# Spreading routing weights by one f32r product per slot, and a split wait in the feed-forward blocks

## Chip, cores and metric

One core of one Trainium2 chip. The metric is the device time of one execution in microseconds (us), measured three times for the kernel before. The five engines are TensorE (PE, with its weight loads shown as PEld), VectorE (DVE), ScalarE (ACT), GpSimd (POOL) and SyncE (SP). Each runs its own instructions in order and waits for others by semaphores.

## The reference

Four layers stand behind each other, each with a layer norm and added to its input: windowed attention, a feed-forward network (FFN) with routed low-rank parts, a state-space mixer, and the same FFN again. x has 1024 tokens of 256 values. The FFN is what the change touches:

```python
gate_logits = einsum('bsd,ed->bse', x, gate_w)          # 8 experts
topw, sel = top_k(gate_logits, 2)
topw = softmax(topw, axis=1)                            # over the tokens, not over the two
base_up, base_gate = xt @ w_up.T, xt @ w_gate.T         # 704 hidden
for e in range(8):
    c = sum(where(sf == e, wf, 0.0), axis=1)            # weight of a token for this expert
    h_e = silu(base_up + lo_up[e]) * (base_gate + lo_gate[e])   # lo_*: rank 16
    ch = c[:, None] * h_e
    mixed_h += ch
    lora_down += 2.0 * (ch @ down_A[e].T @ down_B[e].T)
out = mixed_h @ w_down.T + lora_down
```

Everything is float32.

## The kernel before

The kernel doesn't loop over experts: each token has two slots (its two chosen experts), and all work is done for slot 0 and slot 1. Values lie transposed, with hidden units on the 128 partitions and tokens in the columns, in two halves of 512 tokens (HALF). The 704 hidden units are HB = 6 blocks; the last is half full, and its up and gate products share one bank. So an FFN has N = 12 steps i = 6 * half + block. Precision is kept by splitting each float32 operand in a high and a low f32r part and adding three products (`three`).

What a step does, by engine:

- PE: `base_x(i)` makes the up products (6 of 512 columns, into bank i % 2) and the gate products (6 more, into bank 2 + i % 2); for the half-full block there is one group of 6. `base_lora(i)` adds the low-rank part of slot 0 (3 + 3 products), then signals `a`. `second(i)` adds, on top, the low-rank part of slot 1 less that of slot 0, once slot 0 has been read (`t0`), and signals `b`. `down(i)` is the product with the down weights.
- ACT: `silu(i, s)` reads the up bank into f_sil (signals `sil0`, `sil1`), and copies high parts.
- DVE: `gated(i, s)` multiplies the gate bank with f_sil into f_t (signals `t0`, `t1`); then f_t times the routing weight f_wb gives f_ch; low parts are differences. In the first FFN, ACT and DVE also split the weights as they come in (`split`, pieces 0 to 7; block b needs piece b + 1).

The steps overlap. The queue of PE in iteration i is `base_x(i)`, `base_lora(i)`, `second(i - 1)`, `down(i - 2)`; `base_x(i)` waits for `t1` of step i - 2, which used the same banks. After the loop, PE goes on with early products of the mixer.

The start of an FFN is written out by hand. The masks of slot 0 and slot 1 (`masked(h, n)`, n = 0 to 7: 0 to 3 for slot 0, 4 and 5 for the up part of slot 1, 6 and 7 for its gate part) are multiplied by DVE into f_um and counted by `um`. Between them, DVE, PE and ACT hand each other the steps of the softmax over the tokens; it ends with DVE's WT, one column for each pair of slot and group of 128 tokens, with the tokens on the partitions. The weight of each token is wanted in all partitions, along the columns. `weigh(h)` on PE does that, with WT's column repeated as the stationary operand and the identity as the moving one, four products of 128 columns for each slot and half, in plain float32. ACT copies the result from PSUM to f_wb (`weights_out`). `weigh(0)` stands behind `second(0)`, `weigh(1)` behind `base_x(2)`.

The mixer later in the program does a thing of the kind the change brings: it repeats a small tile over 128 columns, splits it (tile cumsum_hl) and has POOL scale it by parameter columns (L2014, L2022).

Of the kernel before, what the change touches and what calls it, by code (L numbers as in the profile page):

```python
# [20 lines left out]
F32 = mybir.dt.float32  # L21
# [63 lines left out]
PR_END = PR_CS + 26  # L85
# [17 lines left out]
def build(nc, ins, out, phases=4):  # L103
    ctx = ExitStack()
    with ctx:
# [166 lines left out]
        def attention():  # L272
# [511 lines left out]
            def banks_free(e):  # L784
# [22 lines left out]
        F_EVENTS = dict(lg=2, lgt=2, lgr=2, lgc=2, m8=NT, ix=NT, ixf=2, hot=4, top_dve=6, top_pe=3, ex=SLOTS,  # L807
                        wb=4, wbc=4, u=4, uhi=4, ulo=4, mk=4, mk0=2, mk1=2, mk2=2, um=16,
                        da=4, dd0=4, dd=4, dh=4, dl=4, y=4, add=4)
        F_EVENTS |= {n: 2 * HB for n in "a b d sil0 sil1 t0 t1 ch0 ch1 mix mxh mxl".split()} | dict(chh=4 * HB, chl=4 * HB)  # L810
        FS = {n: sem(f"ffn_{n}") for n in F_EVENTS}
        TOP_DVE = {n: i + 1 for i, n in enumerate(("mt", "gm", "dg", "nmc", "rs", "wt"))}
        TOP_PE = {n: i + 1 for i, n in enumerate(("mtT", "nm", "sum"))}

        def ffn(tag, first, before):
# [16 lines left out]
            d_hl = at(f"{tag}_d_hl", [P, 2, HALF], F32R, U_CH + 18432)  # L832
            lg = small[:, 0:64]
# [5 lines left out]
            WT = sm[:, 32:48].rearrange("p (k t) -> p k t", k=2)  # L839
# [137 lines left out]
            def base_x(e, i, parts=(0, 1)):  # L977
# [22 lines left out]
            def pe(e):  # L1000
                def second(i):
                    h, b = divmod(i, HB)
                    if b == 0:
                        need(e, "um", 8 * h + 8)
                    need(e, "t0", i + 1)
                    for which in range(2):
                        m = three(e, to_bank(i, which), lambda w: blk(w, b, (FB_UPB, FB_GTB)[which]),
# [30 lines left out]
                base_lora(e, 0)  # L1038
                base_lora(e, 1)
# [60 lines left out]
            def act(e):  # L1100
# [26 lines left out]
                split(3)  # L1127
                a_hi(1, (0,))
# [14 lines left out]
                a_hi(1, (1,))  # L1143
                silu(0, 0)

# [1069 lines left out]
```

## Time and profile before

| | us |
|---|---|
| three timed runs, median (lowest, highest) | 546.32 (546.05, 546.5) |
| the profiled execution | 543.31 |
| its span, first to last instruction | 541.5 |
| busy PE, DVE, ACT, POOL | 517.0, 402.6, 310.8, 127.1 |

The span starts with the attention; the first FFN runs from 206 to about 330 us, the mixer to about 420, the second FFN to the end, with overlaps. The granted TensorE clock is 1.0 of full speed in every slice. Rows of the trace give the start and the duration in us, then engine, source line, operation, tiles written and read; "x12" means that twelve instructions in a row are merged in one row. In brackets stand the engine's idle time before and who ended it. Ends of PE's instructions overlap the next ones, so the distance from start to start is what an instruction costs there.

### The profile page before, as it was taken

What the parts mean: (1) busy time and instruction counts of PE and PEld (TensorE: products, weight loads), DVE (VectorE), ACT (ScalarE), POOL (GpSimd) and SP (SyncE); (2) the same over time, 40 slices, a digit from 0 to 9 for tenths busy, and PEclk for the clock granted to TensorE, in tenths of its full rate; (3) what the DMA queues carried; (4) which work ended last, traced back from release to release, by engine and by line L of the source; (5) the groups of instructions that cost most, each with busy time, mean ns of one, the idle gap of its engine ahead of it and who ended that gap; (6) DMA issues with size and microseconds to landing.
All of it is one profiled execution on the core that took longest, in us unless ns stands there. A gap on an engine that the chain in (4) does not pass through costs nothing. (4 is left out here: it accounts for less than half of the span.)

```text
span 541.5 us, 9132 instructions
## 1 busy us (share of the span) xinstructions
PE 517.0 (95%) x3035; PEld 436.8 (81%) x3037; DVE 402.6 (74%) x899; ACT 310.8 (57%) x768; POOL 127.1 (23%) x272
## 2 busy tenths in 40 slices
PE   5999999999999989999999999999898999999996
PEld 4778899998998977788887888757777778888885
DVE  5625565566566898799987899966886877898767
ACT  3656878588687643573443455889662254443342
POOL 2232424244243310000000004569533100000000
PEclk9999999999999999999999999999999999999999
DMA  7320100000002204000040000000000000000101
GB/s 273 116 79 1 40 2 2 2 0 2 2 2 70 83 1 142 1 1 1 0 137 0 2 1 0 2 0 2 0 1 2 0 1 1 1 1 0 40 1 39
DMA packets 5790, 14.25 MB, mean 26 GB/s; under 512 B 624, under 2 KB 2928, under 8 KB 5744
## 3 DMA queue, kind: packets, MB, share of 16 engines
q1 hardware_dynamic: 5744, 13.66, 7.3%
q8 instruction: 25, 0.41, 0.3%
q14 instruction: 21, 0.17, 0.1%
HBM read 12.61 MB, written 1.05 MB: 25 GB/s over the span
## 5 line engine op out<-in xcount | busy, mean ns | idle before, releaser
L170 PE MATMUL psum<-xT_hl,ffn_w_hl 128*128 128x512 f32 x312 | 77.7, 395 | 0.6 <-DVE f_t L1243 0.4
L170 PE MATMUL psum<-f_um,ffn_w_hl 128*128 128x512 f32 x288 | 72.2, 398 | 1.3 <-DVE f_t L1243 1.3
L170 PEld LDWEIGHTS psum<-xT_hl,ffn_w_hl 128*128 128x128 f32 x312 | 56.2, 188 | 12.2 <-issue 0.9
L170 PEld LDWEIGHTS psum<-f_um,ffn_w_hl 128*128 128x128 f32 x288 | 53.3, 188 | 14.2 <-DVE f_um L1255 2.1
L1140 ACT ACTIVATE f_sil<-psum 128x512 f32<-128x512 f32 (+1 forms) x48 | 28.6, 596 | 60.3 <-PE psum L170 60.0
L170 PE MATMUL psum<-wo_hl,oT_hl 128*128 128x256 f32 x384 | 50.8, 281 | 4.2 <-DVE oT_hl L705 2.6
L699 DVE TENSOR_TENSOR pT_hl<-psum,pT_hl 126x360 fp32r<-126x360 f32 (+1 forms) x44 | 23.6, 537 | 41.4 <-ACT pT_hl L606 41.4
L170 PEld LDWEIGHTS psum<-wo_hl,oT_hl 128*128 128x128 f32 x384 | 47.9, 188 | 7.1 <-DVE oT_hl L705 5.1
L170 PE MATMUL psum<-xT_hl,wq_hl 128*128 128x512 f32 x192 | 52.1, 407 | 0.6 <-ACT qT L572 0.6
L1243 DVE TENSOR_TENSOR f_t<-psum,f_sil 128x512 f32<-128x512 f32 (+1 forms) x48 | 33.2, 691 | 26.2 <-ACT f_sil L1140 25.4
L572 ACT ACTIVATE qT<-psum 128x512 f32<-128x512 f32 x32 | 35.0, 1094 | 29.0 <-PE psum L170 29.0
L1158 ACT ACTIVATE f_ch_hl<-f_ch 128x512 fp32r<-128x512 f32 x48 | 30.2, 630 | 37.0 <-DVE f_ch L1299 36.9
L581 ACT ACTIVATE probs<-probs,small 120x66 f32<-120x66 f32 x120 | 40.7, 349 | 4.2 <-DVE small L682 3.4
L170 PEld LDWEIGHTS psum<-xT_hl,wq_hl 128*128 128x128 f32 x192 | 33.9, 189 | 7.7 <-issue 1.7
L170 PEld LDWEIGHTS psum<-ffn_w_hl,f_mix_hl 128*128 128x128 f32 x288 | 36.8, 188 | 3.3 <-DVE x_resid L1342 1.2
L170 PE MATMUL psum<-f_ch_hl,ffn_w_hl 128*128 128x512 f32 x144 | 37.9, 397 | 0.6 <-DVE f_ch_hl L1310 0.6
L170 PE MATMUL psum<-ffn_w_hl,f_mix_hl 128*128 128x256 f32 x288 | 37.7, 280 | 0.5 <-DVE x_resid L1342 0.5
L755 POOL TENSOR_TENSOR probs_wide<-probs,small 120x186 f32<-120x186 f32 x40 | 20.0, 499 | 65.8 <-DVE small L662 65.5
L224 POOL TENSOR_TENSOR ln_rstd<-ln_var_eps,minus_half 128x4 f32<-128x4 f32 x8 | 8.1, 1012 | 113.9 <-DVE ln_var_eps L217 113.9
L1299 DVE TENSOR_TENSOR f_ch<-f_t,f_wb 128x512 f32<-128x512 f32 x48 | 33.2, 691 | 1.4
L170 PEld LDWEIGHTS psum<-f_ch_hl,ffn_w_hl 128*128 128x128 f32 x144 | 26.6, 188 | 7.0 <-DVE f_ch_hl L1310 1.0
L1310 DVE TENSOR_TENSOR f_ch_hl<-f_ch,f_ch_hl 128x512 fp32r<-128x512 f32 x48 | 31.1, 686 | 0.0
(242 smaller groups left out, 1121.4 us busy)
## 6 DMA issues: line engine op xcount, KB each, us to landing
w_raw<-in_wq SPq DMA_DIRECT2D x4, 512.0 KB, 3.3
w_raw<-in_wo SPq DMA_DIRECT2D x4, 512.0 KB, 3.3
ffn_w_raw<-in_ffn SPq DMA_DIRECT2D x3, 576.0 KB, 5.6
ffn_w_raw_far<-in_ffn SPq DMA_DIRECT2D x3, 576.0 KB, 5.2
ssd_w_raw<-in_ssd SPq DMA_DIRECT2D x3, 512.0 KB, 5.7
x_resid<-in_x SPq DMA_DIRECT2D x2, 512.0 KB, 4.4
out_x<-x_resid SPq DMA_DIRECT2D x4, 256.0 KB, 2.2
w_raw<-in_wk SPq DMA_DIRECT2D x1, 512.0 KB, 6.3
```

The lines of the kernel that those rows point to most:

```text
L170: i = e.matmul(dst, lhs(a), rhs(b), start=start and n == 0, stop=stop and n == len(TERMS) - 1, **kw)
L224: e.tensor_tensor(rstd[:, seg], veps[:, seg], minus_half[:, seg], ALU.pow).then_inc(LN["rstd"], 1)
L572: e.activation(qT[:, HALF * half:HALF * half + HALF, h], bank(7 if n == Q_PAIR else 6), ACT.Copy, scale=float(HD) ** -0.5).then_inc(s_qt, 1)
L581: m = e.activation(p[:, n, :], p[:, n, :], ACT.Exp, bias=NEGM[0:rows, u % 4, n:n + 1], accum_out=DEN[0:rows, u % 4, n:n + 1])
L699: e.tensor_tensor(pT_hl[0:nk, u % 2, LO, 0:n], bank(2 + u % 2)[0:nk, 0:n], f32(pT_hl[0:nk, u % 2, HI, 0:n]), ALU.subtract).then_inc(s_plo, 1)
L755: e.tensor_tensor(wide, p[:, :, SINK:KBLK], spread(r, KB_WIN), ALU.mult)
L1140: e.activation(sil[at_rows, s, :], bank(i % 2)[rows, :], ACT.Silu).then_inc(FS[f"sil{s}"], 1)
L1158: e.activation(ch_hl[:, i % 2, s, HI, :], ch[:, i % 2, s, :], ACT.Copy).then_inc(FS["chh"], 1)
L1243: e.tensor_tensor(tt[rows, s, :], to_bank(i, 1)[rows, :], sil[rows, s, :], ALU.mult).then_inc(FS[f"t{s}"], 1)
L1299: e.tensor_tensor(ch[:, i % 2, s, :], tt[:, s, :], wb[:, s, half(h)], ALU.mult).then_inc(FS[f"ch{s}"], 1)
L1310: e.tensor_tensor(ch_hl[:, i % 2, s, LO, :], ch[:, i % 2, s, :], f32(ch_hl[:, i % 2, s, HI, :]), ALU.subtract).then_inc(FS["chl"], 1)
```

## The change

`weigh` no longer makes eight plain float32 products for a half, but one f32r product of 512 columns for each slot. What it needs is made in new steps: DVE writes the 16 weight columns eight times beside each other (`w_rep`, 128x128). PE transposes that into bank 7, so that tokens lie in the columns and each partition holds one pair of slot and token group, repeated. ACT copies it rounded to f32r (`wr`), and DVE puts the low part into every other quarter of 32 partitions. ACT (half 0) and POOL (half 1) scale it by parameter columns that keep a partition's row only for its own token group (`wr_rhs`). The stationary operand (`slot_rows`) keeps the rows of a slot, so that the product sums high and low part over the partitions into all 128 of them. `pack` adds ten parameter columns.

DVE's queue at the start changes: `masked(0, 4, 5)`, then the new low part, `gated(0, 0)`, and only then `masked(0, 6, 7)`; `second(0)` waits for masks 4 and 5 before its up products and for 6 and 7 before its gate products. `base_x(i)` no longer waits for `t1` before all of its products, but before the up products for `sil1` of step i - 2 (except where that step is the half-full block) and before the gate products for `t1`.

In the mixer, two semaphores are merged into others to make room, with the counts moved on.

```diff
@@ events
-        TOP_DVE = {n: i + 1 for i, n in enumerate(("mt", "gm", "dg", "nmc", "rs", "wt"))}
-        TOP_PE = {n: i + 1 for i, n in enumerate(("mtT", "nm", "sum"))}
+        TOP_DVE = {n: i + 1 for i, n in enumerate(("mt", "gm", "dg", "nmc", "rs", "wt", "wlo"))}
+        TOP_PE = {n: i + 1 for i, n in enumerate(("mtT", "nm", "sum", "wT"))}
@@ base_x (PE)
-                if i >= 2:
-                    need(e, "t1", i - 1)
                 for which in parts[:1] if b == HB - 1 else parts:
+                    if i >= 2:
+                        need(e, "t1" if which or (i - 2) % HB == HB - 1 else "sil1", i - 1)
                     for k in range(KB):
@@ second (PE)
-                        need(e, "um", 8 * h + 8)
+                        need(e, "um", 8 * h + 6)
                     need(e, "t0", i + 1)
                     for which in range(2):
+                        if b == 0 and which:
+                            need(e, "um", 8 * h + 8)
@@ weigh (PE)
-                    need(e, "top_dve", TOP_DVE["wt"])
+                    need(e, ("wr0", "wr1")[h], 1)
                     if h:
                         need(e, "wbc", 2)
                     for s in range(SLOTS):
-                        for i in range(HT):
-                            t = HT * h + i
-                            m = e.matmul(bank(wb_bank(h, s))[:, i * P:(i + 1) * P],
-                                         WT[:, s, t:t + 1].broadcast_to([P, P]), ident, start=True, stop=True)
-                        m.then_inc(FS["wb"], 1)
+                        e.matmul(bank(wb_bank(h, s)), slot_rows[:, s, :], wr_rhs[:, h].rearrange("p t n -> p (t n)"),
+                                 start=True, stop=True).then_inc(FS["wb"], 1)
@@ pe
                 base_lora(e, 0)
+                need(e, "top_dve", TOP_DVE["wt"])
+                e.transpose(bank(7)[:, 2 * P:3 * P], w_rep, ident).then_inc(FS["top_pe"], 1)
                 base_lora(e, 1)
                 second(0)
                 weigh(0)
@@ act
                 split(3)
+                for n in range(SLOTS):
+                    e.activation(slot_rows[:, n, :], ones, ACT.Copy, scale=par[:, WR_SLOT + n:WR_SLOT + n + 1])
                 a_hi(1, (0,))
@@ act
                 a_hi(1, (1,))
+                need(e, "top_pe", TOP_PE["wT"])
+                e.activation(wr, bank(7)[:, 2 * P:3 * P], ACT.Copy).then_inc(FS["wrh"], 1)
                 silu(0, 0)
+                need(e, "top_dve", TOP_DVE["wlo"])
+                for t in range(HT):
+                    m = e.activation(wr_rhs[:, 0, t, :], f32(wr), ACT.Copy, scale=par[:, WR_HALF + t:WR_HALF + t + 1])
+                m.then_inc(FS["wr0"], 1)
@@ dve
-                e.tensor_tensor(WT, EX, spread(RS, NT), ALU.mult).then_inc(FS["top_dve"], 1)
-                masked(0, 4, 5, 6, 7)
+                copies = P // (SLOTS * NT)
+                wide = [P, copies, SLOTS, NT]
+                e.tensor_tensor(w_rep.rearrange("p (q k t) -> p q k t", q=copies, k=SLOTS),
+                                EX.rearrange("p (o k) t -> p o k t", o=1).broadcast_to(wide),
+                                RS.rearrange("p (o k u) -> p o k u", o=1, u=1).broadcast_to(wide),
+                                ALU.mult).then_inc(FS["top_dve"], 1)
+                masked(0, 4, 5)
+                need(e, "wrh", 1)
+                e.scalar_tensor_tensor(out=wr, in0=f32(wr), scalar=par[:, CS_LO:CS_LO + 1], in1=bank(7)[:, 2 * P:3 * P],
+                                       op0=ALU.mult, op1=ALU.add).then_inc(FS["top_dve"], 1)
                 gated(0, 0)
+                masked(0, 6, 7)
                 split(3)
                 gated(0, 1)
@@ pool
                 ln["rstd"](e, 1)
+                need(e, "top_dve", TOP_DVE["wlo"])
+                for t in range(HT):
+                    m = e.tensor_scalar(wr_rhs[:, 1, t, :], f32(wr), par[:, WR_HALF + HT + t:WR_HALF + HT + t + 1], None,
+                                        ALU.mult)
+                m.then_inc(FS["wr1"], 1)
@@ mixer (one of several places of the kind)
-                e.tensor_copy(second(HI), f32(second(LO))).then_inc(S["dtw"], 1)
+                e.tensor_copy(second(HI), f32(second(LO))).then_inc(S["wl"], 1)
...
-                                AX.X, ALU.add).then_inc(S["dtv"], 1)
-                e.wait_ge(S["dtv"], 1)
+                                AX.X, ALU.add).then_inc(S["dt_dve"], 1)
+                e.wait_ge(S["dt_dve"], 1)
```

## Rows read from the trace of the kernel before

**Rows 1.** PE's waits (total, times, longest); a window: length, busy PE, PEld, DVE, ACT.
```profile
PE psum L170 <- DVE f_t L1243: 1.8, 3, 0.7
...
237.00:246.00 9.00, 9.00 (x46) 7.55 (x45) 8.77 (x20) 4.91 (x9) 0.00 (x0) 1.00 0.00 0
```

**Rows 2.** Timeline of PE: start, us, engine, line, what, count, idle before.
```profile
223.17 3.05 PE L170 MATMUL psum<-f_um,ffn_w_hl 128*128 128x512 f32 x12
...
226.88 1.64 PE L170 MATMUL psum<-f_um,ffn_w_hl 128*128 128x512 f32 x6 [0.66 <-DVE f_t L1243]
...
230.06 3.01 PE L170 MATMUL psum<-xT_hl,ffn_w_hl 128*128 128x512 f32 x12
...
232.91 1.95 PE L1018 MATMUL psum<-const_f,softmax_small 128*128 128x128 f32 x16
...
234.61 3.04 PE L170 MATMUL psum<-f_um,ffn_w_hl 128*128 128x512 f32 x12
...
439.54 1.63 PE L170 MATMUL psum<-f_um,ffn_w_hl 128*128 128x512 f32 x6 [0.66 <-DVE f_t L1243]
```

**Rows 3.** Shapes of the new steps: timeline rows and, without a start, groups by form.
```profile
223.55 0.18 DVE L1283 TENSOR_TENSOR softmax_small<-softmax_small 128x16 f32<-128x16 f32 x1
...
350.88 0.35 DVE L1884 SCALAR_TENSOR_TENSOR cumsum_hl<-cumsum_hl,params,psum 128x128 fp32r<-128x128 f32 x1
...
219.63 0.27 PE L1031 MATMUL psum<-const_f,softmax_small 128*2 128x128 f32 x1
...
L1809 ACT ACTIVATE b_tok<-psum 128x128 f32<-128x128 f32 x8 | 2.2, 271 | 0.0
...
376.07 1.30 ACT L1826 ACTIVATE state_decayed<-state,ssd_small 128x128 f32<-128x128 f32 x4
...
L2014 POOL TENSOR_SCALAR cumsum_rhs<-cumsum_hl,params 128x128 fp32r<-128x128 f32 x4 | 1.7, 452 | 0.2 <-DVE ssd_small L1886 0.2
```

**Rows 4.** Timeline of ACT and DVE around block 0 of the first FFN.
```profile
223.64 2.49 DVE L1255 TENSOR_TENSOR f_um<-f_us,f_mT 128x512 fp32r<-128x512 f32 x4
...
224.85 0.60 ACT L1140 ACTIVATE f_sil<-psum 128x512 f32<-128x512 f32 x1 [0.32 <-PE psum L170]
226.05 0.69 DVE L1243 TENSOR_TENSOR f_t<-psum,f_sil 128x512 f32<-128x512 f32 x1
226.65 1.35 DVE L878 TENSOR_TENSOR ffn_w_hl<-ffn_w_raw,ffn_w_hl 128x1152 fp32r<-128x1152 f32 x1
...
228.56 0.60 ACT L1140 ACTIVATE f_sil<-psum 128x512 f32<-128x512 f32 x1 [3.10 <-PE psum L170]
229.19 0.69 DVE L1243 TENSOR_TENSOR f_t<-psum,f_sil 128x512 f32<-128x512 f32 x1 [1.19 <-ACT f_sil L1140]
```

**Rows 5.** Timeline of POOL and DVE in the mixer.
```profile
369.61 1.57 POOL L1971 TENSOR_SCALAR xs_D<-xs,params 128x512 f32<-128x512 f32 x1
...
372.81 1.05 POOL L2046 TENSOR_TENSOR x_dt_decay<-x_dt,decay 128x512 f32<-128x512 f32 x1
...
373.48 0.94 DVE L1908 TENSOR_TENSOR g_lo<-gated,g_hi 128x512 fp32r<-128x512 f32 x1 [1.87 <-ACT g_hi L1838]
373.84 2.00 POOL L1971 TENSOR_SCALAR xs_D<-xs,params 128x512 f32<-128x512 f32 x1
```

**Rows 6.** Timeline, further on in both FFNs: DVE's gaps and PE's next waits.
```profile
236.04 0.69 DVE L1318 TENSOR_TENSOR f_mix_hl<-f_mix,f_mix_hl 128x512 fp32r<-128x512 f32 x1 [0.31 <-ACT f_mix_hl L1169]
...
253.62 0.69 DVE L1243 TENSOR_TENSOR f_t<-psum,f_sil 128x512 f32<-128x512 f32 x1 [0.45 <-ACT f_sil L1140]
...
271.77 0.69 DVE L1243 TENSOR_TENSOR f_t<-psum,f_sil 64x512 f32<-64x512 f32 x1
...
272.91 2.89 PE L170 MATMUL psum<-xT_hl,ffn_w_hl 128*128 128x512 f32 x12
...
300.75 3.00 PE L170 MATMUL psum<-xT_hl,ffn_w_hl 128*128 128x512 f32 x12 [0.43 <-DVE f_t L1243]
...
457.94 0.69 DVE L1243 TENSOR_TENSOR f_t<-psum,f_sil 128x512 f32<-128x512 f32 x1 [2.18 <-ACT f_sil L1140]
```

More of the change, by code:

```diff
@@ L84 @@
 CS_LO, CS_RA, CS_RB, CS_LA, CS_LB, CS_FIRST = (PR_CS + n for n in (0, 1, 5, 9, 17, 25))
-PR_END = PR_CS + 26
+PR_WR = PR_CS + 26
+WR_HALF, WR_SLOT = PR_WR, PR_WR + NT
+PR_END = PR_WR + NT + SLOTS
 GW_PARTS = 2 * KB * EXPERTS
@@ L832, in ffn @@
             d_hl = at(f"{tag}_d_hl", [P, 2, HALF], F32R, U_CH + 18432)
+            wr = at(f"{tag}_weight_rows", [P, P], F32R, A_W + 16384)[:, :]
+            w_rep = at(f"{tag}_weights_repeated", [P, P], F32, A_W + 16896)[:, :]
+            slot_rows = at(f"{tag}_slot_rows", [P, SLOTS, P], F32R, A_W + 17408)
+            wr_rhs = at(f"{tag}_weight_rows_rhs", [P, 2, HT, P], F32R, A_W + 20480)
             lg = small[:, 0:64]
@@ L1470, in mixer @@
             dst = lambda b: cb_pre[:, :] if b == 0 else xs[:, b - 2, :]
-            names = ("xda dtw dtv cs cm rhs mb sel gs da raw wh wl bcz ip tap ipz part carry join cv sl xd dt dt_dve dt_pool dt_act de L G xt X xdd wt ce Y St st1 st y g ghi glo g2 ss "
+            names = ("xda cs cm rhs mb sel gs da raw wh wl bcz ip tap ipz part carry join cv sl xd dt dt_dve dt_pool dt_act de L G xt X xdd wt ce Y St st1 st y g ghi glo g2 ss "
                      "ve ri O fin bt").split()
@@ L1520, in mixer @@
             W_ORDER = ("0", "out", "z", "c")
+            WL_ORDER = ("0", "dt", "out", "z", "c")
             def w_hi0(e):
@@ L1571, in in_proj @@
                 if b == 1:
-                    e.wait_ge(S["dtw"], 1)
+                    e.wait_ge(S["wl"], WL_ORDER.index("dt") + 1)
                     for k in range(KB):
@@ L1696, in project @@
                     if c == 0:
-                        e.wait_ge(S["wl"], W_ORDER.index("out") + 1)
+                        e.wait_ge(S["wl"], WL_ORDER.index("out") + 1)
                     if c >= 2:
@@ L1777, in act @@
                 last_tap(11)
-                e.wait_ge(S["dt_dve"], 2)
+                e.wait_ge(S["dt_dve"], 3)
                 e.activation(E1, AV, ACT.Exp, scale=-1.0).then_inc(S["dt_act"], 1)
@@ L1869, in dve @@
                 e.tensor_reduce(t3(V), bank(7)[:, 0:NT * DT_ROWS].rearrange("p (t w h) -> p t h w", t=NT, w=2),
[L1870 to L1871 removed]
+                                AX.X, ALU.add).then_inc(S["dt_dve"], 1)
+                e.wait_ge(S["dt_dve"], 1)
                 e.tensor_tensor(t3(V), t3(V), repeat(par[:, PR_DTB:PR_DTB + NH], NT), ALU.add).then_inc(S["dt_dve"], 1)
[L1873 removed]
+                e.wait_ge(S["dt_dve"], 2)
                 e.scalar_tensor_tensor(out=AV, in0=V, scalar=-1.0, in1=V, op0=ALU.mult,
@@ L1987, in join @@
                     e.tensor_tensor(out, out, carry[:, b, :], ALU.add).then_inc(S["join"], 1)
-                e.wait_ge(S["dt_dve"], 2)
+                e.wait_ge(S["dt_dve"], 3)
                 step(e.tensor_scalar(RL, V, 0.0, None, ALU.max))
@@ L1996, in pool @@
                 step(e.tensor_scalar(AN, AN, -1.0, None, ALU.mult))
-                e.wait_ge(S["dt_dve"], 3)
+                e.wait_ge(S["dt_dve"], 4)
                 step(e.tensor_tensor(SP, R1, E1, ALU.mult))
@@ L2152, in cumsum_parts @@
     later, lo = (quarter >= 2)[:, None], (quarter % 2 == 1)[:, None]
-    return np.concatenate([-1.0 * lo, at_head * ~later, at_head * later, -at_chunk * later, at_chunk * ~later, 1.0 * ~later],
-                          1).astype(np.float32)
+    at_tile = (k[:, None] % 32 < SLOTS * NT) * ~later * (k[:, None] % NT == np.arange(NT)[None, :])
+    at_slot = 1.0 * (k[:, None] // NT % SLOTS == np.arange(SLOTS)[None, :])
+    return np.concatenate([-1.0 * lo, at_head * ~later, at_head * later, -at_chunk * later, at_chunk * ~later, 1.0 * ~later,
+                           at_tile, at_slot], 1).astype(np.float32)
 def pack(i):
```

11 lines of the change are left out of this document (5 added, 6 removed).

## Prediction

> **What bounds the kernel now.** I read the waits of TensorE first, then its busy time by windows, then the order of time around each place that the diff touches. In the first feed-forward network (FFN) PE is busy without a gap from 237 to 246 us, and DVE is nearly as full: 8.77 of 9 us. PE waits for DVE's gate product (f_t) three times in the program, 1.8 us in all [rows 1]. So time taken from PE's queue in an FFN shortens the program as long as DVE can follow; where DVE is full, it can not. Two of the three waits stand at the place that the change edits, 0.66 us each, before block 0's second-slot products at 226.88 and 439.54 [rows 2]. The second FFN repeats the first 212.66 us later there.
>
> **The products that spread the weights.** Before, `weigh` runs eight plain fp32 products of 128 columns for one half. The second one starts at 232.91 and the next products at 234.61: 1.70 us of PE's queue. After, it is two f32r products of 512 columns. Twelve of that kind take 230.06 to 232.91, so 0.2375 us each, 0.48 for two [rows 2]. Saved: 1.22 us in each of four calls, if PE is what is late there.
>
> **What makes the rows.** Each step is priced by the row of its shape; none of them is in the program before at this place.
> - DVE writes 128 columns (`w_rep`) instead of 16, which took 0.18: between 0.18 and the 0.35 of a 128x128 STT [rows 3]. I take 0.28, so the masked products start at 223.74 instead of 223.64.
> - PE transposes it behind `base_lora(0)`: 6 of the 12 products that begin at 223.17, so at 224.65; a single such transpose lasted 0.27 [rows 2, 3], done 224.92. It lies in PE's idle 0.66.
> - ACT copies it: 0.27 as the b_tok row [rows 3], up to 0.60 as a 128x512 one [rows 4]. Until 225.2. `silu(0,0)`, queued behind, runs 225.2 to 225.8; before, it began at 224.85 [rows 4].
> - DVE makes the low parts, 0.35 [rows 3], 225.26 to 225.61, after `masked(0,4,5)`. `gated(0,0)` follows at 225.81 instead of 226.05, because two of the four masked products (0.62 apart) are now behind it. It ends at 226.50.
> - ACT's four scaled copies: 1.30 us for four [rows 3], 225.8 to 227.1. ACT was idle until 228.56 [rows 4], and `weigh(0)` comes later still: nothing. If that cover were gone, 1.3 us on PE. The two for `slot_rows`, 0.65 by the same row, stand earlier, where ACT waits for `lora_a`'s products: nothing.
> - POOL's four: 0.45 each at most, 1.8 us for one FFN [rows 3], 225.65 to 227.4, wanted at 232.5: nothing on the path, but see below.
>
> **Block 0's second slot.** The up half can start at 226.64 (0.14 behind DVE, as 226.74 to 226.88 before), but the gate half now waits for masks 6 and 7, which DVE runs behind `gated(0,0)`: from 226.43 they would end at 227.74. Here POOL interferes. In the mixer DVE's g_lo, with both inputs in SBUF, came at 373.48 while a POOL product ran from 372.81 to 373.86, and took 0.94 instead of the 0.69 of other 128x512 products [rows 4]; it ended 0.56 after POOL's. The POOL instruction behind it took 2.00 against 1.57 for its like [rows 5]. The masked products have both inputs in SBUF too. So POOL's third copy falls between masks 6 and 7, and mask 7 ends 0.56 after its end of 227.43: at 228.0. The bounds are 227.74 (no effect) and 228.5 (two POOL copies in the way); I take 228.0, as the g_lo row is the nearest. The Trainium skill says the same of it ("SBUF — State Buffer", Who interferes with whom): such a DVE instruction and a GpSimd one that reads SBUF exclude each other for a whole instruction. The trace agrees, 0.94 against 0.69 us; without that rule the sum would be 0.26 us better in each FFN.
>
> Then the gate half starts at 228.12, and its results are there at 229.01 (second products of 226.88 were at 228.5, by the silu at 228.56). `silu(0,1)` runs 229.05 to 229.65, against 228.56 before. `base_x(2)` started at 230.06; its up part now waits for that silu alone and starts at 229.79, 0.27 earlier; its gate part needs `gated(0,1)` (229.68 to 230.37) at 231.2. With the old wait it would start at 230.51, 0.45 later than before. So the new wait is worth 0.7 us here: the deferred masks cost it and it buys them back. DVE's low part of weight piece 3, queued in front of `gated(0,1)`, was 226.65 to 228.00 and ends near 229.6, in time.
>
> A wait between up and gate products costs PE nothing when it is met: the 12 products of slot two have one in their middle and still take 3.0 us [rows 2].
>
> **Second FFN.** 0.27 and then 1.22 at `weigh(1)`: PE is 1.49 us ahead. DVE was idle for 2.18 us before 457.94 [rows 6], so it follows. (The second `weigh(0)` saving is within the 0.27: PE waits for the silu there.) **1.5 us.**
>
> **First FFN.** PE is 1.49 ahead after `weigh(1)` too, but DVE also splits weights and is 0.49 late at `gated(0,1)` (229.68 for 229.19). It has few gaps to make that up: 0.31 before 236.04 (the ACT copy of mix, which comes early now), 0.45 before 253.62, both filled, and some 0.2 in gaps too short to be printed. At `gated(5,1)`, 271.77 before, it is then 0.27 to 0.47 early. Block 5 shares one bank, so `base_x(7)` still waits for that product: before at 272.91, now 271.77 + 0.69 + 0.14 less 0.27 to 0.47, 272.13 to 272.33 [rows 6]. So 0.58 to 0.78 is left of 1.49; I take 0.7. At the other `base_x` before it the new wait (silu) is early enough. From there DVE has gaps and follows. At 300.75 PE waited 0.43 for f_t because layer-norm statistics stand in front of it on DVE; the up part now waits for the silu in front of those, so this 0.43 goes [rows 6]. **1.1 us.** The mixer behind it is a chain that starts with this output, so it moves as a whole.
>
> The renamed mixer semaphores (dtw into wl, dtv into dt_dve) fire at the same instructions, and the ten more columns of parameters are 5 KB at the start: nothing.
>
> **Sum.** 1.1 + 1.5 = 2.6 us. The profiled execution, 543.31 us (span 541.5 and 1.8 around it), goes to 540.7. It was 3.0 below the median of the three timed runs, 546.32, so the prediction is 546.32 - 2.6 = 543.7.
>
> **Rivals.**
> - No interference of POOL: mask 7 at 227.74, 0.26 more in each FFN: 543.2. For it: the order of arrival may let POOL finish first. Against: [rows 5]. 0.17.
> - DVE doesn't hold PE in the first FFN (it gets back 0.8 us more than I count): 1.5 + 0.43 + 1.5 = 3.4 to 3.9 with the first rival, 542.7. 0.06.
> - DVE takes all of it: it stays late until block 5, only the 0.43 and the second FFN are left, 1.9: 544.4. [rows 6] allow it if the ACT copy of mix doesn't come early. 0.12.
> - The change doesn't do what it says: the new round trip PE, ACT, DVE stands in DVE's queue ahead of `gated(0,0)` and takes d longer; everything up to `base_x(2)` is late by d in both FFNs, 2.6 - 2d. With the 128x512 durations for all three steps (0.69, 0.60, 0.69) d is 1.06, and 545.8 comes out: no change. 0.10.
> - Slower: the same trip, with POOL or a queue adding to it so that d passes 1.3, where the gain is used up (low parts ready after 226.9); past 1.85 the loss is over 0.2%, and at 2.0 it is 547.7. Against it: a hand-off from PE to ACT took 0.05 us here (228.51 to 228.56), and there are three. 0.05.
>
> **Chances.** Forecast 0.5 (543.4 to 544.1), rivals as above. A measurement of this kernel can tell about 0.2%, 1.1 us, from no change. Faster 0.5 + 0.17 + 0.06 + 0.12 = 0.85, same 0.10, slower 0.05. The range leaves out the last two cases and the best half of the second: 542.6 to 545.2.
>
> **What would show it.** Right: two PE products of 0.24 instead of 1.70 us in each `weigh`; low parts ready near 225.6; mask 7 lengthened beside a POOL copy; `base_x(2)` released by a silu near 229.8; a PE wait for f_t before `base_x(7)` near 272.2 in the first FFN and none in the second; no wait at 300. Wrong: low parts after 226.9; gates of block 0 held beyond 228.5; new PE waits for f_ch_hl or f_mix_hl in either FFN; `base_x(7)` without a wait.

## The result, and the profile after

| | before | after |
|---|---|---|
| median of six timed runs (lowest to highest) | 545.10 (543.54 to 546.5) | 539.69 (538.94 to 540.4) |
| ratio of the times, 95% interval | | 0.9905 (0.9881 to 0.9928) |
| the profiled execution, and its span | 543.31, 541.5 | 540.40, 538.6 |
| busy PE, DVE, ACT, POOL | 517.0, 402.6, 310.8, 127.1 | 513.9, 402.8, 313.4, 134.4 |

The kernel became faster, by 5.4 us of the medians. The prediction said 2.6 us faster, 543.7 us, with a range from 542.6 to 545.2. The time lies below the range by 2.9 us.

The busy times of the page give the first reading.

```profile
span 538.6 us, 9048 instructions
...
PE 513.9 (95%) x2981; PEld 431.7 (80%) x2983; DVE 402.8 (75%) x901; ACT 313.4 (58%) x782; POOL 134.4 (25%) x280
```

PE lost 3.1 us of work, ACT took on 2.6 and POOL 7.3. The span is 2.9 shorter. But these two executions can't be laid beside each other from time zero. PE's rows at the start, before and then after (start, duration, engine, line, what, count), show why:

```profile
9.44 3.31 PE L415 MATMUL psum<-const_f 128*128 128x256 f32 x12
12.59 2.10 PE L170 MATMUL psum<-xT_hl,wk_hl 128*128 128x512 f32 x8
```

```profile
9.48 4.68 PE L417 MATMUL psum<-const_f 128*128 128x256 f32 x12
13.82 1.04 PE L172 MATMUL psum<-xT_hl,wk_hl 128*128 128x512 f32 x3
```

Twelve products on constants, the same in both kernels, took 3.31 us before and 4.68 after: in the trace's clock records the full clock (2.4 GHz) is granted from 10.6 us before and from 13.4 us after, with PE busy without a gap since 7.7 in both. (The page prints full clock ahead of these moments too, where it has no record; the same products stand 0.43 us apart there and 0.22 behind them.) So the first product of the attention begins 1.23 us later. Of the change only the ten parameter columns, loaded at the start, stand ahead of it, and in the traces of the experiments this product begins anywhere from 12.68 to 14.13, in the kernels with these columns from 12.68 to 13.95, in those without from 13.57 to 14.13. So **every "earlier" and "later" below is taken against the first wk product of the same trace**: 1.23 is subtracted from the times of after. By that measure the change is worth 4.07 us in the trace, and not 2.9:

| place | before | after, less 1.23 | difference |
|---|---|---|---|
| block 0, slot two, up half | 226.88 | 226.53 | -0.35 |
| the same, gate half | 227.66 | 227.73 | +0.07 |
| base_x(2) | 230.06 | 229.47 | -0.59 |
| first product behind weigh(1) | 234.61 | 232.78 | -1.83 |
| base_x(7) | 272.91 | 271.25 | -1.66 |
| base_x of step 10 | 300.75 | 298.60 | -2.15 |
| first product of the mixer | 321.43 | 319.13 | -2.30 |
| second FFN's first masked product | 435.83 | 433.64 | -2.19 |
| last product of the program | 537.87 | 533.80 | -4.07 |

The order of time around block 0 of the first FFN in the kernel after, PE alone, answers to [rows 2]:

```profile
225.81 0.27 PE L1045 MATMUL psum<-const_f,f_weights_repeated 128*128 128x128 f32 x1
...
227.76 0.93 PE L172 MATMUL psum<-f_um,ffn_w_hl 128*128 128x512 f32 x3 [0.28 <-DVE f_t L1258]
228.96 0.96 PE L172 MATMUL psum<-f_um,ffn_w_hl 128*128 128x512 f32 x3 [0.27 <-DVE f_um L1270]
229.76 0.62 PE L1024 MATMUL psum<-f_weight_rows_rhs,f_slot_rows 128*128 128x512 f32 x2
230.70 3.01 PE L172 MATMUL psum<-xT_hl,ffn_w_hl 128*128 128x512 f32 x12 [0.32 <-ACT f_sil L1149]
233.55 0.62 PE L1024 MATMUL psum<-f_weight_rows_rhs,f_slot_rows 128*128 128x512 f32 x2
234.01 2.96 PE L172 MATMUL psum<-f_um,ffn_w_hl 128*128 128x512 f32 x12
```

Read the six second-slot products first. Their one wait of 0.66 has become two of 0.28 and 0.27, the second of them for the deferred masks. Then `base_x(2)`, at 230.70, waits for the silu, as the new semaphore says, and its twelve products have no gap in the middle: the gate part never waited for DVE. Last, `weigh(1)`: from 233.55 to 234.01 is 0.46 us, where it was 1.70 [rows 2].

The same stretch on ACT, DVE and POOL in the kernel after answers to [rows 4]:

```profile
224.71 0.29 DVE L1300 TENSOR_TENSOR f_weights_repeated<-softmax_small 128x128 f32<-128x128 f32 x1
...
226.43 0.35 DVE L1306 SCALAR_TENSOR_TENSOR f_weight_rows<-f_weight_rows,params,psum 128x128 fp32r<-128x128 f32 x1 [0.22 <-ACT f_weight_rows L1154]
226.92 0.69 DVE L1258 TENSOR_TENSOR f_t<-psum,f_sil 128x512 f32<-128x512 f32 x1
227.53 1.38 DVE L1270 TENSOR_TENSOR f_um<-f_us,f_mT 128x512 fp32r<-128x512 f32 x2
228.83 1.34 DVE L884 TENSOR_TENSOR ffn_w_hl<-ffn_w_raw,ffn_w_hl 128x1152 fp32r<-128x1152 f32 x1
230.59 0.69 DVE L1258 TENSOR_TENSOR f_t<-psum,f_sil 128x512 f32<-128x512 f32 x1 [0.41 <-ACT f_sil L1149]
```

```profile
226.12 0.28 ACT L1154 ACTIVATE f_weight_rows<-psum 128x128 fp32r<-128x128 f32 x1 [0.42 <-PE psum L1045]
...
226.81 1.28 ACT L1158 ACTIVATE f_weight_rows_rhs<-f_weight_rows,params 128x128 fp32r<-128x128 f32 x4
```

```profile
226.88 4.27 POOL L1423 TENSOR_SCALAR f_weight_rows_rhs<-f_weight_rows,params 128x128 fp32r<-128x128 f32 x4 [15.43 <-DVE f_weight_rows L1306]
```

The round trip (PE's transpose 225.81, ACT's copy 226.12, DVE's low parts 226.43) has steps of 0.31 us. It is done at 226.78, 225.55 against the first wk product, where 225.6 was forecast. The two deferred masks, 227.53 to 228.91, are hardly longer than without POOL: singly 0.68 and 0.78. POOL's four copies took 4.27 together; singly 0.61, 1.14, 1.98 and 0.60. So POOL and DVE do get in each other's way, but it is POOL that gives way.

PE's list of waits (total, times, longest) answers to [rows 1], where f_t held PE for 1.8 us in three waits:

```profile
PE psum L172 <- ACT f_sil L1149: 0.6, 2, 0.3
...
PE psum L172 <- DVE f_t L1258: 0.6, 2, 0.3
PE psum L172 <- DVE f_um L1270: 0.5, 2, 0.3
```

The sum is nearly the same, 1.7 us: waits were exchanged, and PE reaches them earlier. The wait at step 10, 0.43 in [rows 6], is gone:

```profile
299.83 2.89 PE L172 MATMUL psum<-xT_hl,ffn_w_hl 128*128 128x512 f32 x12
```

### The profile page after: what moved, and what is told of

Same layout as the page of the kernel before. It is cut to its first block and busy times, and to the rows that moved or that the text cites. A ratio compares the mean times of both kernels' runs of the same rounds, so it can differ in the third digit from the quotient of the medians.

```text
span 538.6 us, 9048 instructions
## 1 busy us (share of the span) xinstructions
PE 513.9 (95%) x2981; PEld 431.7 (80%) x2983; DVE 402.8 (75%) x901; ACT 313.4 (58%) x782; POOL 134.4 (25%) x280
## 5 line engine op out<-in xcount | busy, mean ns | idle before, releaser
L172 PEld LDWEIGHTS psum<-xT_hl,ffn_w_hl 128*128 128x128 f32 x312 | 56.1, 188 | 13.4 <-DVE ffn_w_hl L884 1.3
```

What stands on the lines that cost most here:

```text
L172: i = e.matmul(dst, lhs(a), rhs(b), start=start and n == 0, stop=stop and n == len(TERMS) - 1, **kw)
```

## The experiments

Each edit is given against the kernel it starts from. "Earlier" is against the first wk product of the trace; for the second FFN, it is against that FFN's first masked product, so that its own share is seen. Two questions were open. Which part of the change brought the 4.07 us of the trace, where 2.6 were counted? And where do the other 1.3 us between the medians (5.4) come from? The timed runs of the kernel before beside the experiments gave a hint on the second: they fall in two groups. In 28 of 59 the mean granted clock was 0.996 or 0.997, and their mean time is 546.27; in the other 31 it was 0.999 or 1.0, and their mean is 543.90.

**The old wait, with all the rest of the change.** Edit, to the kernel after:

```diff
+                if i >= 2:
+                    need(e, "t1", i - 1)
                 for which in parts[:1] if b == HB - 1 else parts:
-                    if i >= 2:
-                        need(e, "t1" if which or (i - 2) % HB == HB - 1 else "sil1", i - 1)
```

> The changed kernel with the old wait put back: all products of base_x(i) wait for t1 of step i - 2. In the changed kernel base_x(2) starts 0.14 us behind the silu of slot 1; gated(0,1) ends 0.58 us behind that silu's end, so with the old wait each FFN starts base_x(2) 0.7 us later. Theory A (DVE doesn't hold PE in the first FFN, the split wait is worth its 0.7 in both FFNs and 0.5 at the layer-norm statistics of the first): 1.9 us slower than the changed kernel. Theory B (the first FFN is held by DVE at base_x(7) whatever PE does before): 0.7 + 0.5 = 1.2 us slower, and a longer wait of PE for f_t at base_x(7) in the changed kernel than here.

Measured: 544.17 us (543.24 to 544.6, ten runs), ratio to before 0.9981 (0.9962 to 1.0). PE in this kernel:

```profile
229.50 0.62 PE L1024 MATMUL psum<-f_weight_rows_rhs,f_slot_rows 128*128 128x512 f32 x2
231.16 2.98 PE L172 MATMUL psum<-xT_hl,ffn_w_hl 128*128 128x512 f32 x12 [1.04 <-DVE f_t L1258]
...
240.75 1.61 PE L172 MATMUL psum<-xT_hl,ffn_w_hl 128*128 128x512 f32 x6 [0.54 <-DVE f_t L1258]
```

`base_x(2)` now waits 1.04 instead of 0.32 us, and later, at 240.75, a `base_x` that didn't wait in either kernel waits 0.54: PE has run ahead of DVE and the old wait ties it back. The mixer starts 0.58 us earlier than before instead of 2.30, and the second FFN gains 1.21 of its own instead of 1.88. So **in this kernel the split wait is worth 1.72 + 0.67 = 2.4 us**. The forecast had put 0.7 on it at `base_x(2)`, and it let the 0.43 at step 10 go with it: 1.8 with both FFNs, as in theory A; the 2.4 are more, and further still from the 1.2 of theory B. The median is 4.5 above that of after, 2.1 more than the waits explain; all ten runs showed a clock of 0.996 or 0.997. That is the second question, taken up below.

**The split wait alone.** Edit, to the kernel before: the reverse of the diff above.

> The kernel before with the split wait alone. base_x(2) can't start earlier, as the plain products of weigh(0) end at 230.06; only the waits of 0.43 and 0.1 us at steps 10 and 11 of the first FFN go. Both theories: 0.4 to 0.5 us faster than before, and the second FFN starts and ends the same. A rival, that a second wait inside base_x costs PE some time at each of 16 steps, gives 0 or slower.

Measured: 545.4 us (542.81 to 545.72, ten runs), ratio 0.9996 (0.9974 to 1.0018). In the trace nothing moves until step 10, where the 0.43 goes (the step starts 0.61 earlier); the mixer starts 0.77 us earlier, more than the 0.4 to 0.5 expected, and the second FFN gains nothing. So a second wait inside `base_x` costs PE nothing that shows. The medians are no measure of so little, since eight of the ten runs belong to the lower-clock group; the mean of these eight is 0.8 below that of before's lower-clock runs (545.48 against 546.27), and the two others are 1.0 below the mean of its group (542.87 against 543.90). Both agree with the trace.

**The masks for both halves ahead of the new steps.** Edit, to the kernel after:

```diff
-                masked(0, 4, 5)
+                masked(0, 4, 5, 6, 7)
...
                 gated(0, 0)
-                masked(0, 6, 7)
```

> The changed kernel with masks 6 and 7 back in front of gated(0,0), right behind 4 and 5, and in front of the low part of the weight rows. gated(0,0) would start 0.78 us later, the up half of the second-slot products with it, but the gate half follows at once: its results come 0.3 us later, and so base_x(2), in each FFN. If DVE doesn't hold PE: 0.6 us slower than the changed kernel, 0.3 in each FFN. If POOL's copies cost DVE time when they meet the masks, as I forecast (0.26 us), they no longer meet them, and the loss is only 0.1 in each.

Measured: 540.46 us (539.9 to 540.84, five runs), ratio 0.9919 (0.9887 to 0.995). PE in this kernel:

```profile
227.22 1.63 PE L172 MATMUL psum<-f_um,ffn_w_hl 128*128 128x512 f32 x6 [0.94 <-DVE f_t L1258]
...
229.64 2.99 PE L172 MATMUL psum<-xT_hl,ffn_w_hl 128*128 128x512 f32 x12 [0.32 <-ACT f_sil L1149]
```

The up half starts 0.57 later than in the kernel after, but the gate half only 0.14 later, and `base_x(2)` only 0.05: -0.54 against before, where the kernel after has -0.59. At the mixer the two differ by 0.02, in the second FFN by 0.05. The silu of slot two waits for the whole of the second-slot products. In the kernel after, the last three of them follow the last mask; here all six follow `gated(0,0)`, which stands behind the masks in DVE's queue, and they end at nearly the same time. So the deferral brings some 0.1 us in each FFN at most, which traces can't tell from zero, and not the 0.3 expected without interference. The four runs here without a low clock have a mean of 540.22, 0.4 above that of the kernel after (539.8, below); the traces show no such difference, and five runs are too few to make one of it. The prediction let the deferral cost something and the split wait buy it back; no cost of it is seen.

**The split wait and the deferred masks, with the old products.** Edit, to the kernel before: the split wait, and in DVE's queue and in `second`

```diff
-                masked(0, 4, 5, 6, 7)
+                masked(0, 4, 5)
                 gated(0, 0)
+                masked(0, 6, 7)
...
-                        need(e, "um", 8 * h + 8)
+                        need(e, "um", 8 * h + 6)
...
+                        if b == 0 and which:
+                            need(e, "um", 8 * h + 8)
```

> The kernel before with the split wait and the deferred masks, but with WT and the eight plain fp32 products of weigh kept. The weight rows, their transpose and copies are left out. By the rows of before: results of the second-slot products of block 0 come 0.12 us earlier, base_x(2) 0.1 us earlier, 0.5 at the steps 10 and 11: 0.7 us faster than before in all. The rest of the changed kernel's gain, 4.1 us in the trace from the first low-rank products on, is then the new products': 3.4 us.

Measured: 545.01 us (542.46 to 545.7, ten runs), ratio 0.9994 (0.9973 to 1.0015). In the trace `base_x(2)` is 0.05 later than before, the mixer 0.70 earlier, the second FFN 0.13 faster: 0.83 in all. With the two first experiments the parts can be laid out, in us of the trace:

| | first FFN (to the mixer) | second FFN | sum |
|---|---|---|---|
| split wait alone | 0.77 | 0.00 | 0.77 |
| split wait, deferred masks | 0.70 | 0.13 | 0.83 |
| new products, deferred masks, old wait | 0.58 | 1.21 | 1.79 |
| all three | 2.30 | 1.88 | 4.18 |

(The sum of the last row is not 4.07, because the mixer gives 0.11 back.) 0.77 and 1.79 make 2.56, and both together 4.18. On top of the split wait the new products with the deferred masks bring 4.18 - 0.77 = 3.4 us, and with the old wait 1.79. They take time out of PE's queue, and the split wait keeps DVE from taking it back.

**After once more.** No edit; more runs, for the clock.

> The changed kernel itself, beside the kernel before on one chip, to see its granted clock in many executions. The kernel before has three groups of times so far: near 543.5 and 544.4 us (clock 1.000 and 0.999) and near 546.3 (clock 0.997, 12 of 26), the last with the clock at its lower level for 3.4 us at the start of the second FFN. Theory C: the work moved by the change is worth 4.1 us, as the trace from the first low-rank products on shows, and the rest of the 5.4 us between the medians is this dip, which the changed kernel's executions seldom fall into because PE's gap at the end of the mixer comes 2.2 us earlier. Then this kernel lies between 538.9 and 540.4 with clock 0.999 or 1.000 in most executions. Theory D: the dip is chance, alike for both, and 6 without one were luck (0.54 to the 6th, 0.02): near half of these executions would be near 542.4 at clock 0.997.

Measured: 540.23 us (539.05 to 540.57, six runs), ratio 0.9911 (0.9887 to 0.9936). Of twelve executions of the kernel after, these and the first six, one had a mean clock of 0.997 (540.57), where before had 28 of 59. The other eleven have a mean of 539.8. Against before's mean of 543.90 at the same clock that is 4.1 us, the 4.07 of the trace. Theory C fits; by theory D near half of the executions would have the low clock. The profiled execution of this run also shows how far such differences repeat: by the same rule its last product is 4.31 earlier than before's, the mixer 2.37 and the second FFN 1.97, where the first trace of after has 4.07, 2.30 and 1.88. Differences between traces of less than about 0.2 us are left out of the conclusions below, save where one row shows them.

Where the clock goes shows in the windows of the kernel with the old wait, at the end of the mixer and the start of the second FFN (stretch, length, busy PE, PEld, DVE, ACT, POOL, then the granted clock as a share of full speed):

```profile
416.00:418.00 2.00, 0.97 (x9) 0.74 (x7) 1.72 (x5) 1.67 (x4) 0.00 (x0) 1.00 0.04 8
418.00:420.00 2.00, 2.00 (x16) 2.00 (x16) 1.34 (x4) 0.00 (x0) 0.55 (x1) 0.81 0.00 0
420.00:422.00 2.00, 2.00 (x7) 1.61 (x7) 1.01 (x4) 0.00 (x0) 0.55 (x1) 0.50 0.00 0
422.00:424.00 2.00, 2.00 (x9) 1.61 (x8) 1.77 (x5) 0.10 (x1) 0.00 (x0) 0.83 0.00 0
```

PE was busy for 0.97 of 2 us, waiting for the residual at the end of the mixer. Then, though PE is full, the granted clock is 0.50 of full speed, which is the lower of its two levels, 1.2 GHz, for about 3.4 us: (0.19 + 0.50 + 0.17) x 2 / 0.5. From the mixer's start to the second FFN's first masked product this kernel loses 1.56 us, and the other three traces with such a dip 1.58 to 1.65.

**That gap filled, in the kernel before.** Edit: five products on constants, 512 columns each, into bank 3, by the helper that the kernel uses in other gaps of the mixer.

```diff
                     if i == NT + 1:
                         early(phase, "tr0", e)
+                        keep_busy(5, 3)
```

> The kernel before with five bf16 products of 512 columns more on PE, into the spare bank 3, behind the early transposes of the second FFN, where PE waits 1.03 us for x_resid in the mixer's end (0.97 us busy of the 2 from 416 to 418). They take 5 times 0.21 = 1.05 us, the length of the gap, so they add 0.1 at most. If the gap is what makes the clock fall: no execution at 0.997, all times between 543.2 and 544.5, the median 1.3 to 2 us under that of the kernel before where half of its executions dip. If the dip has another cause: two groups as before.

Measured: 544.18 us (543.4 to 544.89, twelve runs), ratio 0.9986 (0.997 to 1.0002). None of the twelve runs had a clock below 0.999. The windows of this kernel:

```profile
416.00:418.00 2.00, 1.95 (x16) 1.49 (x15) 0.84 (x2) 1.50 (x3) 0.53 (x1) 1.00 0.00 0
418.00:420.00 2.00, 2.00 (x16) 1.70 (x15) 1.93 (x5) 0.61 (x2) 0.00 (x0) 1.00 0.00 0
420.00:422.00 2.00, 2.00 (x14) 1.78 (x13) 1.27 (x7) 0.00 (x0) 0.55 (x1) 1.00 0.00 0
```

PE is busy through the gap and the dip doesn't come; apart from that the trace is that of before to 0.2 us. **So the gap leads to the dip.** What decides in which executions of one and the same program it comes was not tested by a run; the last section has what the clock records say of it.

**The gap filled, with the old wait.** Edit: the same line, to the kernel of the first experiment.

> The changed kernel with the old wait (all ten executions at clock 0.996 or 0.997, 544.2 us) and the five filling products. If its 4.5 us over the changed kernel are 1.9 to 2.3 us of waiting and the rest the dip, it comes to 541.5 to 542.3 us at clock 0.999 or 1.000. If the old wait costs 4.5 by itself, it stays at 544.

Measured: 541.99 us (541.54 to 542.91, ten runs, all at a clock of 1.0), ratio 0.9948 (0.993 to 0.9965). The first experiment had 544.17, so 2.2 us went with the dip. What is left over the kernel after, 2.3, is what its trace has: the mixer 1.72 later than after, and 1.12 won in the second FFN where after has 1.88. That puts the split wait at 2.3 us in time, and at 2.4 to 2.5 in the traces.

**The gap filled, in the kernel after.** Edit: the same line.

> The changed kernel with the five filling products at the end of the mixer. 11 of its 12 executions had no dip of the clock, so the filling can only take away the one of twelve: the same 539.0 to 540.6 us, none at clock 0.997. If the filling costs time of its own, it shows here: the same kernel without a dip is the reference.

Measured: 539.75 us (539.07 to 540.6, six runs, none below 0.999), ratio 0.9903 (0.9878 to 0.9928). No difference to after, whose runs hardly ever had the dip; the filling products cost nothing.

**The second silu ahead of the gate half.** The prediction found the silu of slot two to release `base_x(2)`. In the kernel after it waits for all of the second-slot products, though it reads the up bank alone. Edit, to the kernel after, with a new semaphore `bu`:

```diff
@@ second (PE)
+                        if b == 0 and which == 0:
+                            m.then_inc(FS["bu"], 1)
@@ silu (ACT)
-                    need(e, "ab"[s], i + 1)
+                    if s and i % HB == 0:
+                        need(e, "bu", i // HB + 1)
+                    else:
+                        need(e, "ab"[s], i + 1)
@@ gated (DVE)
+                    if s and i % HB == 0:
+                        need(e, "b", i + 1)
```

> The changed kernel where the silu of slot 1 of block 0 (and block 0 of the second half) no longer waits for the gate half of the second-slot products, but for the up half, which is done 1.2 us earlier; gated(0,1) waits for the gate half itself. In the changed kernel PE is idle 0.32 us before base_x(2) for that silu. It would be done while the gate half runs, so base_x(2) follows weigh(0) at once: 0.3 us earlier in each FFN, or 0.45 with the delay that the trace shows behind weigh. 0.6 to 0.9 us faster than the changed kernel if DVE doesn't hold the first FFN, 0.3 to 0.5 if it does.

Measured: 539.45 us (538.76 to 541.24, six runs, two of them with the dip), ratio 0.9912 (0.9885 to 0.9939). PE in this kernel:

```profile
229.13 0.61 PE L1026 MATMUL psum<-f_weight_rows_rhs,f_slot_rows 128*128 128x512 f32 x2
229.60 3.03 PE L172 MATMUL psum<-xT_hl,ffn_w_hl 128*128 128x512 f32 x12
```

No wait is left at `base_x(2)`; it stands 0.58 earlier than in the kernel after. The mixer starts 0.70 earlier. In the second FFN 0.57 is won behind `weigh(1)`, but only 0.18 of it reaches the end. PE's wait for f_ch_hl there, late in that FFN, shows where the rest went:

```profile
PE psum L172 <- DVE f_ch_hl L1341: 0.9, 1, 0.9
```

It was 0.6 us in the kernel after. At the end DVE's last products are late, and PE only comes earlier to wait for them. In all the last product is 0.9 us earlier than in the first trace of the kernel after and 0.6 earlier than in the second; the four runs without the dip have a mean of 539.16, 0.6 below that of the kernel after. Expected were 0.6 to 0.9.

**The same, with the gap filled.** Edit: both.

> The early silu and the filling products together. Without a dip the early silu gave 538.8 to 539.7 us, with it (2 of 6) 541.2. Expected: all executions between 538.7 and 540.0, 0.7 to 0.9 us under the changed kernel with the filling, none at clock 0.997.

Measured: 538.57 us (538.27 to 540.0, six runs, all at a clock of 1.0), ratio 0.9888 (0.9863 to 0.9914). It is the lowest median of all kernels here, 1.1 us below after, and four of the six runs lie below the range expected. The traces show less: the last product is 0.55 us earlier than in the kernel after with the gap filled. How much of the rest is the start of the attention (first wk product at 12.68 here, at 13.95 there) is not separated.

**POOL's copies behind the deferred masks.** Edit, to the kernel after:

```diff
                 need(e, "top_dve", TOP_DVE["wlo"])
+                need(e, "um", 8)
                 for t in range(HT):
```

> The changed kernel where POOL's four copies wait until all eight masks of the first half are written, so that they meet none of them. In the changed kernel mask 7 took 0.78 us beside POOL's second copy, mask 6 0.68, and POOL's copies 1.14 and 1.98 us against 0.61 of the first. If DVE gives way to POOL as I had forecast, the masks gain 0.26 us or more here; if POOL gives way to DVE, mask 7 gains 0.1 and the gate half of block 0 starts 0.1 us earlier in each FFN, 0.2 us in all, and POOL's copies are still lengthened, by the split of weight piece 3 behind the masks.

Measured in one run: 540.23 us. POOL and PE in this kernel:

```profile
228.98 3.31 POOL L1424 TENSOR_SCALAR f_weight_rows_rhs<-f_weight_rows,params 128x128 fp32r<-128x128 f32 x4 [17.57 <-DVE f_um L1270]
```

```profile
228.85 0.96 PE L172 MATMUL psum<-f_um,ffn_w_hl 128*128 128x512 f32 x3 [0.17 <-DVE f_um L1270]
```

Without POOL beside them the two masks take 1.28 instead of 1.38 us, and the wait before the gate half is 0.17 instead of 0.27. By these rows POOL's part in DVE's time is 0.1 us for each FFN, and not 0.26. At the mixer and over the second FFN (0.05 and 0.14 us in the trace) it is within what repeats of after differ by. The copies, now beside DVE's split of the weights, still take 3.31 instead of 2.4 (four of 0.60).

## Why the prediction was right and wrong

**The first product and its price: right.** Two products took 0.46 us (0.48 forecast), and in both FFNs PE is 1.24 us further ahead behind `weigh(1)` (1.22 forecast).

**The new steps: right.** `w_rep` took 0.29 (0.28), the transpose 0.27, ACT's copy 0.28 (0.27), the low parts 0.35, ACT's four copies 1.28 (1.30). Only POOL's four were priced wrong: 4.27 us instead of 1.8 at most, since one alone takes 0.60 and two were lengthened. They end at 231.15, 229.9 against the first wk product, ahead of the 232.5 where they are wanted, so nothing waits for them. The rival of the long round trip, and the slower one that rests on the same trip, are refuted: d is nil.

**The interference of POOL: wrong side.** The term "mask 7 at 228.0" had DVE pay 0.26 for POOL's copies, after [rows 5], where a DVE product came while a POOL instruction was 0.67 us under way, and waited. That row was read rightly: the next three of its kind in the mixer, at 378.61, 384.77 and 391.27, also come into a POOL instruction and end 0.54 or 0.55 behind it. Here, with DVE's instructions back to back, mask 7 took 0.78 for 0.68, and POOL's second and third copy 1.14 and 1.98 for 0.60. The Trainium skill's rule ("SBUF — State Buffer", Who interferes with whom), by which the one that issues first goes through and the other stands, fits both places only if DVE's instructions, back to back here, mostly won the turn; no run shows the moment of issue itself. `base_x(2)` was to come 0.27 earlier, 0.53 without interference, and came 0.59. The rival without interference was right in this term, worth 0.32 in the first FFN and 0.25 in the second.

**The split wait: right in kind, too small.** I said that it is worth 0.7 at `base_x(2)` and gives back the 0.43 at step 10. At `base_x(2)` it was 0.65 in the first FFN and 0.72 in the second, taken from the kernels with and without it. But I took it for a local gain, and counted it as buying back the deferral. With the old wait PE is tied to DVE at each `base_x`, and loses more, 0.54 at 240.75 among it. (The row by which I found a wait in the middle to cost nothing, 234.61, is six products of slot 0 and six of slot 1, not twelve of slot two; the finding holds, 3.01 us for the twelve at 230.70.)

**DVE as the limit of the first FFN: the step that failed.** I let 0.7 us of 1.49 get to `base_x(7)`, because DVE was to be 0.49 late at `gated(0,1)` and to have 0.96 us in gaps to make up. It came 1.66 earlier. Both terms were off. DVE was 0.17 late (230.59 less 1.23, for 229.19). And between that product and block 5's, it made up 1.53. The windows between the two, of the kernel before and of the one after (the third busy time is DVE's), say how:

```profile
229.19:271.77 42.58, 42.58 (x229) 35.86 (x229) 40.58 (x69) 22.75 (x37) 0.00 (x0) 1.00 0.01 2
```

```profile
230.59:271.64 41.05, 40.94 (x210) 34.10 (x211) 39.99 (x70) 22.16 (x37) 0.55 (x1) 1.00 0.03 7
```

Before, DVE was idle for 2.00 us (42.58 - 40.58), after for 1.06. These 0.94 are the 0.96 that I had counted, printed gaps and small ones. What I left out is the other 0.59, by which its busy time (the time in which at least one instruction runs) fell for the same work. DVE's instructions that follow each other without a wait begin before the one ahead has ended: of the rows above, f_t of 226.92 lasts 0.69, and f_um begins 0.61 behind it. So a gap that closes gives back more than its length. The 0.31 of [rows 6] shows it, before and then after:

```profile
234.44 1.29 DVE L1310 TENSOR_TENSOR f_ch_hl<-f_ch,f_ch_hl 128x512 fp32r<-128x512 f32 x2
```

```profile
235.78 1.29 DVE L1334 TENSOR_TENSOR f_ch_hl<-f_ch,f_ch_hl 128x512 fp32r<-128x512 f32 x2
236.99 0.68 DVE L1342 TENSOR_TENSOR f_mix_hl<-f_mix,f_mix_hl 128x512 fp32r<-128x512 f32 x1
```

From the start of the f_ch_hl pair to that of f_mix_hl (236.04 before) it is 1.60 us before and 1.21 after: 0.39 for a gap of 0.31. By the records of single instructions, three closed gaps (0.31, 0.45, 0.14) give 1.15, and five more places, where DVE had waited a little without a gap, 0.05 to 0.07 each. The product with the half-full bank, 271.64, still releases `base_x(7)`, as forecast: 271.64 + 0.69 + 0.14 is 272.47, and it started at 272.48, which is 271.25 against the first wk product, where 272.2 was forecast. PE was 1.89 us ahead at `base_x(6)`, 1.66 there, 1.56 at `base_x(9)`; at step 10, where the 0.43 went as said, it was 2.15. So DVE held PE by 0.3 us, where the forecast had it take 0.8. First FFN: 1.1 forecast, 2.30 measured at the mixer (2.15 before it), near to the rival in which DVE doesn't hold PE, to which I gave 0.06 because I had counted gaps without the overlap.

**Second FFN: right in kind, short.** 1.49 forecast; 0.52 + 1.24 = 1.76 behind `weigh(1)`, and 1.88 at the end. The rest is POOL's 0.25 and the last stretch, 0.12.

**The reference: an unexplained difference left standing.** I saw that the profiled execution of before, 543.31, was 3.0 below the median of the three timed runs, took it as given, and subtracted the gain of one from the time of the other. The 3.0 are mostly two things that vary between executions: the dip of the clock behind the mixer's gap, 1.6 us in the traces that have it, and the start of the attention, up to 1.5. By their times, 546.05 to 546.5, the three runs lie in the group with the dip (545.3 to 546.6); their clock is not on record. In 28 of 59 later executions it was there; in the kernel after it was in 1 of 12. The median of before's six runs, 545.10, lies between the groups, 1.2 above the mean of the group without the dip. So 1.2 of the 5.4 us is that the dip has become rare, which no row of the profiled execution of before could show: it has no dip. The change doesn't remove the gap: the kernel after has the same one (1.03 us ahead of the row at 415.84), and the kernel with the old wait had the dip in ten runs of ten. It moves it; see the last section. Measured from the profiled execution the forecast was 540.7, and that of after took 540.4, but this agreement is chance: the later start, 1.23, hides as much as the trace gained beyond the sum, 1.5.

In numbers, for the gain: forecast 2.6; first FFN +1.2, second +0.4, mixer -0.1, which gives the 4.07 of the trace; the clock +1.2; what is left, 0.1, is within the scatter of the medians. For the time: 543.7 was 4.0 too high, 1.5 by the sum and 2.4 by the reference (546.32 against 543.90), with 0.1 left.

## What to carry to other kernels

A wait for the last of several things, ahead of a group of products, should be split so that each product waits for what it reads: alone it may bring next to nothing (0.77 us here), and it decides how much a cut in the queue ahead of it is worth (the new products bring 1.8 us without it, 3.4 on top of it). When an engine that looks full is to catch up, its gaps are not all that it can give back: add the overlap of the instructions that come to stand back to back (0.9 us of gaps and 0.6 of overlap here). When the profiled execution and the timed ones differ by more than their scatter, find out which stretch differs before the sum is set against either.

## What the hardware showed beyond that

- **A small gap can cost clock, in some executions only.** PE has some 1.03 us without work at the end of the mixer, in an otherwise full stretch. In four traces about 3.4 us at 1.2 GHz with PE busy follow it, for 1.6 us of time; the mean clocks of 0.996 and 0.997 in 28 of 59 executions of the kernel before are of that size (3.4 us at half in 542). With five products on constants in the gap, none of 34 executions (four kernels) had it. Of the variants that left the gap, ten of ten, eight of ten, nine of ten, two of six, one of five and one of twelve had it, though the gap is alike in all.
- **What seems to decide is how far the gap lies behind the first full clock.** In the four traces with the dip the gap begins 402.89 to 403.38 us after the clock records first show full clock, and the dip begins 406.19 us after it in every one. In the five traces with the gap and no dip, the gap begins at 401.44, 401.60, 402.19 and 402.22 (the kernel after and two variants of it) and at 405.32 (the kernel before). The change moves the gap 2.3 us earlier against the first wk product, which would make the dip rare without removing its cause. Nine traces fit this; no run moved the gap alone, so it is not shown.
- **The start of the attention varies by 1.5 us** between executions (first wk product at 12.59 to 14.13), as the full clock is granted earlier or later to the same products on constants (3.31 to 4.78 us for twelve). The Trainium skill ("TensorE: Matmul & The Clock Gate", Part 1) says that the length of the slow start changes from run to run of the same kernel; the traces agree.
- **DVE's instructions overlap when nothing is between them**, 0.61 from start to start for a duration of 0.69 (226.92 and 227.53).
- **A POOL copy of 128x128 to f32r with one scalar takes 0.60 us**, more than the 0.45 with two scalars in [rows 3], and up to 1.98 beside DVE instructions with both inputs in SBUF; of the two masks beside it one lost 0.1, and the split of the weights behind them nothing (1.34 for 1.35).
